# Four strips to a turn in place of two in the loops of all three stages of a vision-tower kernel

## What is computed

```python
h = tok(x)                      # 8x8 windows, 8 heads of 8, rotary positions, softmax, projection
h = h + attn(layernorm(h))      # 8 heads, each token sees a 7x7 neighbourhood of the 64x64 grid
h = h + ffn(layernorm(h))       # routed + shared experts, two layers, relu
h = h + ret(layernorm(h))       # causal linear attention with decay 0.99
h = h + bin(layernorm(h))       # gated sum of 8 weights, sign(x) @ sign(w), scaled
```

## Time and profile before

| | us |
|---|---|
| three runs | 1687.75, 1695.73, 1697.24 |
| median | 1695.73 |
| the profiled execution's own time | 1688.66 |
| its span, first to last instruction | 1686.8 |
| PE busy | 1561.1 |
| DVE busy | 1205.0 |
| ACT busy | 1048.7 |
| POOL busy | 610.4 |

### The profile page before, as it was taken

One profiled execution on the slowest core, in us unless ns is written; L12 is line 12 of the kernel. 1 busy time (PEld: TensorE's weight loads), 2 busy tenths in 40 slices (PEclk: granted clock), 3 DMA queues, 4 the chain that ended last, 5 costly groups with the idle time before them and its releaser, 6 DMA issues.

```text
span 1686.8 us, 83309 instructions
## 1 busy us (share of the span) xinstructions
PE 1561.1 (93%) x29546; PEld 1164.2 (69%) x29546; DVE 1205.0 (71%) x3605; ACT 1048.7 (62%) x2053; POOL 610.4 (36%) x923
## 2 busy tenths in 40 slices
PE   5899999879999999999976999999999999999996
PEld 3677777657877887887754666676666766666663
DVE  1566566547888888888756778787787787877862
ACT  2565656434555555555422678788888888888876
POOL 4243232155766666666623222122221222222210
PEclk9999999969999999999986999999999999999998
DMA  3201010034444444454410333333333333333332
GB/s 104 82 25 31 25 31 25 19 93 113 130 124 132 127 129 129 126 133 129 131 50 22 84 80 87 83 83 88 83 84 86 83 88 83 81 89 83 85 77 58
DMA packets 134833, 143.15 MB, mean 85 GB/s; under 512 B 42770, under 2 KB 90258, under 8 KB 134514
## 3 DMA queue, kind: packets, MB, share of 16 engines
q1 hardware_dynamic: 126450, 116.07, 26.7%
q10 hardware_dynamic: 8320, 26.22, 5.5%
HBM read 66.42 MB, written 16.99 MB: 49 GB/s over the span
## 4 chain that ended last, share of the span: by engine, by line
PE 81%; issue 5%; DVE 5%; SPq 3%; ACT 3%; DMA 1%; POOL 1%; DVEq 0%; ACTq 0%; POOLq 0%
PE ps_D L900 12%; PE ps_D L811 8%; PE ps_OT L830 4%; DVE prob L1486 4%; PE ps_D L687 4%; PE ps_AV L838 3%; PE ps_AV L917 3%; SPq L465 3%; PE ps_D L807 3%; PE ps_OT L764 2%; PE ps_J L1008 2%; PE ps_J L976 2%; PE ps_J L958 2%; PE ps_OT L653 2%; PE ps_J L1039 2%
## 5 line engine op out<-in xcount | busy, mean ns | idle before, releaser
L1210 ACT ACTIVATE prob<-ps_D 128x1024 bf16<-128x1024 f32 x448 | 459.5, 1029 | 121.0 <-PE ps_D L900 119.3
L1180 ACT ACTIVATE prob<-ps_D 100x512 f32<-100x512 f32 x256 | 139.0, 595 | 103.8 <-PE ps_D L811 103.8
L560 POOL TENSOR_TENSOR tile_a<-q_st,q_mask 128x512 f32<-128x512 f32 x128 | 135.2, 1056 | 144.7 <-PE ps_D L811 138.0
L811 PE MATMUL ps_D<-tile_a,key_patch 64*100 64x128 f32 x2048 | 175.4, 290 | 0.0
L900 PE MATMUL ps_D<-tile_a,w_parts 128*128 128x256 bf16 x1024 | 153.3, 275 | 11.9 <-DVE xg L1523 3.7
L900 PE MATMUL ps_D<-tile_b,w_parts 128*128 128x256 bf16 x1024 | 152.7, 274 | 11.9 <-DVE xg L1523 2.9
L1372 DVE TENSOR_REDUCE m_sb<-ps_D 128x4 f32<-128x400 f32 x256 | 134.6, 566 | 25.6 <-PE ps_D L788 25.3
L534 POOL TENSOR_TENSOR rstd_bin<-veps_bin,minus_half 128x2 f32<-128x2 f32 x64 | 44.1, 689 | 266.9 <-DVE veps_bin L1271 266.9
L534 POOL TENSOR_TENSOR rstd_ret<-veps_ret,minus_half 128x2 f32<-128x2 f32 x64 | 46.5, 727 | 250.7 <-DVE veps_ret L1271 250.7
L811 PEld LDWEIGHTS ps_D<-tile_a,key_patch 64*100 64x100 f32 x2048 | 134.2, 167 | 0.1
L900 PEld LDWEIGHTS ps_D<-tile_a,w_parts 128*128 128x128 bf16 x1024 | 92.9, 103 | 45.4 <-issue 33.9
(11 more groups left out here) (183 smaller groups left out, 4027.5 us busy)
## 6 DMA issues: line engine op xcount, KB each, us to landing
tile_a<-xg SPq DMA_DIRECT2D x384, 64.0 KB, 2.0
tile_b<-xg SPq DMA_DIRECT2D x384, 64.0 KB, 2.0
key_st<-k_d SPq DMA_DIRECT2D x128, 162.0 KB, 3.1
tile_b<-v_d ACTq DMA_DIRECT2D x128, 120.0 KB
tile_b<-v_d ACTq DMA_DIRECT2D x64, 160.0 KB
w_exp<-experts SPq DMA_DIRECT2D x64, 129.0 KB, 2.3
xT<-in_x SPq DMA_DIRECT2D x32, 256.0 KB, 2.6
k_d<-kpad SPq DMA_DIRECT2D x64, 64.0 KB, 2.9
```

The costliest lines, as they stand in the source:

```text
L560: gp.tensor_tensor(q_block[:, par, :].rearrange("c (p h q) -> c p h q", h=NH, q=NQ)[:, own, :, :], q_st[:, par, :].rearrange("c (p a q) -> ...
L811: mm = pe.matmul(s_loc[x][0:NKL, u * P:(u + 1) * P], key_patch[rows_of(x), par, at * NKL:(at + 1) * NKL], q_block[rows_of(x), par, at * P: ...
L1180: act.activation(prob1[0:NKL, 2 * g + x, :], s_loc[x][0:NKL, :], ACT.Exp).then_inc(T2["exp_done"], 1)
L1210: act.activation(sgn[:, k % 4, :], unit(k, par)[:, :], ACT.Sign).then_inc(BN["sign"], 1)
```

## The change

The three helpers that hold the loops write four strips into a turn where two stood, on every engine that calls them: `pairs` in stage one (loop over pairs 1, 3, ..., 13, each turn does two pairs), `strips_ahead` in stage two (1, 3, ..., 27) and `staggered` in stage three. There the loop now begins at strip 10 and steps by 4 up to 58, so strips 8 and 9 are written out. No step, wait, buffer or order changes.

```diff
         def staggered(eng, strips):
 
-            for j in range(8):
+            for j in range(10):
                 strips(j, j % 2)
-            with eng.Fori(8, NSTRIP - 2, 2) as j:
-                strips(j, 0)
-                strips(j + 1, 1)
+            with eng.Fori(10, NSTRIP - 5, 4) as j:
+                for n in range(4):
+                    strips(j + n, n % 2)
             for j in range(NSTRIP - 2, NSTRIP + 7):
                 strips(j, j % 2)
...
             full = (NSTRIP - LEAD - 1) // 2
-            with eng.Fori(1, full) as j:
-                strip(j, 0)
-                strip(j, 1)
+            with eng.Fori(1, full - 1, 2) as j:
+                for n in range(4):
+                    strip(j + n // 2, n % 2)
             for j in range(full, NSTRIP // 2):
...
             part(0, 0)
             part(0, 1)
-            with eng.Fori(1, NT // 2 - end) as j:
-                part(j, 0)
-                part(j, 1)
+            with eng.Fori(1, NT // 2 - end - 1, 2) as j:
+                for n in range(4):
+                    part(j + n // 2, n % 2)
             for j in range(NT // 2 - end, NT // 2):
```

## The result

The changed kernel takes 1931.0 us (median of four runs, 1917.6 to 1935.5) against 1694.3 us for the kernel before (four runs, 1687.8 to 1697.2): 1.139 times as long, 95% interval 1.1322 to 1.1459. The profiled execution took 1935.5 us, its span is 1933.6. The prediction was 1942 us, +253 over the profiled execution of before; the two profiled executions are 246.8 us apart, the two medians 236.7. Two executions further down, of 2185.6 and 4654.2 us, fell in a slower state of the core and are in none of the medians.

A forecast was written before the change was run, and what follows sets the result against it. PE, busy 93% of the span, was taken as the bound. Refetched code was to add 76.0 us in the first loop and 182.3 in the second, less 5.3 for jumps: +253.0 on 1688.66, 1942 us; range 1780 to 2020.

The forecast's parts named there:

- The main step: First two loops on PE: doubled bodies are fetched anew each turn, as straight code is; +253.0 us, chance 0.55.
- Rival (a): Jumps of the first two loops: all code stays at hand; +2.3 us, 1691 us, chance 0.15.
- rival (b): First two loops: only colliding blocks, a body's head and tail, are fetched; +111 us, 1800 us, chance 0.20.
- The number of packets: PE's instruction queue q8: about 130 packets more than the 42 before, if both loops are fetched each turn.
- The jump itself: Jump back to absent code in the first two loops: PE waits 3.6 us, between 2.6 and 4.6.
- The fetched body: Each old two-strip body now fetched: 3.4 us more in the first loop, 4.2 in the second.
- The clock: After each jump's stop in the first two loops, the lower granted clock costs 1.7 us, half of 3.4.
- The sum by stage: First loop 76.0 us more, second 182.3, third 0, less 5.3 for jumps saved: together +253.0 us.
- Stage three at nothing: Third loop: its doubled body, 3.3 blocks, is shorter than what is kept today, so it costs 0.
- The jumps saved: Fewer jumps give back 1.4 us in the first loop, 3.9 in the second, nothing in the third: 5.3 us.

The follow-up runs named there:

- The runs of stage two with nine blocks needed: Four strips a turn in stage two of the kernel before: 1820.5 us; with 190 semaphore increments ahead, 1867.3 us; with half of L838's matmuls left out, 1756.2 us.
- stage three alone: Kernel before with four strips a turn in stage three only, on all engines: 1695.1 us, 1.0011 times.
- all engines but PE alone: Kernel before with four strips a turn on every engine except PE, which keeps its old loops: 1693.5 us, 0.9997 times.
- stages one and two alone: Two runs, each the kernel before with four strips a turn in one stage: stage one 1787.5 us, stage two 1820.5 us.
- the run with half of the value products: Kernel before with the stage-two change and two of L838's four groups of matmuls left out, so another output: 1756.2 us.

## Why the prediction was right, and where its terms were off

**The main step held.** It was that straight code is the nearest row to a body of this length, so that every turn of the first two loops is fetched anew. q8 brought 195 packets more, 11 in a turn of stage one and 9 in one of stage two: all that the loop touches and the one ahead, each time. Rival (a) asks for 42 to 55 packets in all; rival (b), a fixed place for each block, for 30 to 50 more than before. Both are refuted. The runs of stage two with nine blocks needed show how it comes about: the oldest block leaves first, so a loop that needs nine where eight fit finds none. That a block leaves by the time since it came, and not since it was last used, is not shown: in a loop that runs straight through its blocks both give the same packets. The page "Runtime: NRT & Kernel Launch" of the Trainium skill, "Instruction fetch mechanics", gives PE 2048 instructions in first-in-first-out order; with the 256 to a block measured here that is eight blocks, and the runs agree, as far as they tell one order from another. Its sentence on a window of two pages doesn't hold here: a body that touches seven blocks jumped back eight times and nothing was fetched.

**The number of packets was too low**, about 130 forecast, 195 measured. I took 261 recorded instructions to a block, but waits and register work are in the blocks and not in the views, and the block ahead comes on top: 6 x 11 + 13 x 9 = 183. I took some 20 off for what was fetched anyway, where the longer program adds the other 12.

**The jump itself** was taken as 3.6 us between 2.6 and 4.6. It is 4.0 in stage two and 4.7 in stage one, there just over the upper end. 6 x 1.1 + 13 x 0.4 = 12 us too little.

**The fetched body** was 3.4 and 4.2 us for two strips, 6.8 and 8.4 for four, from the first turns of the old loops. Measured is the idle time inside a turn: (10.9 + 8.3) / 6 = 3.2 us in stage one, 39.2 / 13 = 3.0 in stage two. The two are not the same thing. The 4.2 us of stage two's first turn were a stop of 1.73 us and 2.35 us more of PE's busy time, 17.57 against 15.22, at the clock of the earlier trace rows; the views of the two turns, in the columns of the earlier trace rows:

```profile
383.80:403.20 19.40, 17.57 (x444) 14.12 (x442) 12.78 (x37) 8.13 (x20) 10.62 (x18) 0.91 0.36 101
418.40:433.90 15.50, 15.22 (x458) 12.65 (x450) 12.84 (x37) 8.21 (x20) 10.68 (x19) 1.00 0.47 131
```

So the stops alone were forecast at 2 x 1.73 = 3.5 us and measured at 3.0, and the rest of this term was the clock's cost, in the forecast a second time.

**The clock** was taken as 1.7 us a jump, half of the 3.4 us of the earlier trace rows, a stretch that had followed a stop of 1.73 us. PE's busy time for four strips rises from 230.66 / 6.5 = 35.5 us to 266.75 / 6 = 44.5 in stage one, +9.0 a turn, and from 415.62 / 13.5 = 30.8 to 454.96 / 13 = 35.0 in stage two, +4.2; this holds the clock's cost behind all stops of a turn. In stage two 2 x 2.35 + 1.7 = 6.4 us of it were in the forecast, too much; in stage one, whose first turn ran at a granted clock of 1.00, only the 1.7 of the jump was, far too little. I had noted that the stop would be twice as long and still priced the same loss, and in stage one that is the term that was mis-sized most. The length of the stop alone doesn't settle it: the lower level lasted 20.5 us in stage one behind 4.5 us of stop, and 3.4 or 6.8 us in stage two behind 3.7. Why it lasts so long in stage one is open; a second stop, of 1.86 us, falls into it there.

**The sum by stage.** A turn of stage one was to cost 6.8 + 3.6 + 1.7 = 12.1 us more and costs 53.2 - 37.2 = 16.0; a turn of stage two was to cost 8.4 + 5.3 = 13.7 and costs 42.3 - 31.4 = 10.9. So stage one was forecast at 76.0 and measured at 97.9, too cheap by its clock; stage two was forecast at 182.3 and measured at 143.9, too dear by a fetched body that held the clock's cost once more. The errors of -22 and +38 us have opposite signs, and that the total came within 6 us of the profiled execution and 16 of the medians is in part luck.

**Stage three at nothing** held for its loop: 46.6 us for four strips in both kernels. **The jumps saved** (5.3 us) are shown by no run: in the two loops that were to gain, each jump left costs 4 us and more, and stage three alone and all engines but PE alone come out level, as forecast.

**Open:** why after costs 15 us more than stages one and two alone. The places of the stops in stage two differ (L838 twice, or L807 and L784), which a shift of the block edges explains in kind, but no run separates it. Open too is 6 us between the second and the third loop. And when the block ahead is asked for was seen, not explained: in each turn with 90 instructions or more in the last block, in every second with 28.

## What to carry to other kernels

Before a loop body is made longer, count all of the engine's instructions in it, waits and register work too, and divide by the block; on PE at most seven blocks touched keep the one ahead harmless, and one block more costs the whole body, at each turn or at every second one. The gain of fewer jumps was at most 0.3 us each. If a loop near the limit shows "issue" ahead of its first line and instruction packets in its repeating stretch, shorten it, or try to shift it by some instructions. A count made at the recorded jump is too low by the matmuls still queued there, here mostly 10 to 16 instructions.

## What the runs showed of the hardware

- PE keeps eight blocks of 256 instructions (2048) and gives up the oldest. Seven touched and one ahead stay (46 and 43 packets in all, none in the repeating turns), eight touched stay for a turn when the ninth isn't asked for (491.1 to 524.7 us of the run with half of the value products), and where nine are needed nine are fetched, each time that the ninth is asked for. VectorE keeps some 290 instructions, not 550, in blocks of half that size.
- A jump to code that isn't there costs PE 4.0 to 4.7 us on average in the changed kernel, 5.1 on average and up to 5.9 with other block edges, and DVE 3.2 where it could be read. At the edge of a fetched block, where matmuls are short and dense, PE stops: 1.8 us on average before L716, 1.5 before L838 and 0.5 before L703 in the changed kernel.
- The granted clock goes down to 0.50 with such a stop: for 20.5 us with a stop of 4.5 us in stage one, for 3.4 or 6.8 us with one of 3.7 in stage two, and for 3.4 us behind one of 1.7 in the kernel before. In stage one PE's busy time grew by 9.0 us a turn, more than the 7.9 us that PE stood still in it.
- An instruction that only counts a semaphore up takes PE 0.15 us in a row of such: the first matmul starts at 18.18 us behind 62 of them, at 22.47 behind 90, at 37.98 behind 190. The first 10.13 us are waited for a transfer in any case, so 62 delay it by 8.05 us only.
- 60 such instructions at the head of the program, in a kernel whose loop needed one block too many, made it 81 us faster.
